# Second message-passing layer of a graph network: keys spread by a product on TensorE instead of a broadcast load

## The reference

```python
h = relu(layernorm(x))
for W, b, act in ((W1, b1, relu), (W2, b2, identity)):      # two message-passing layers
    fwd = segment_sum(h[src], dst) / max(deg_in, 1)
    bwd = segment_sum(h[dst], src) / max(deg_out, 1)
    h = act(concat([h, fwd, bwd]) @ W + b)
x = x + h
h   = relu(layernorm(x))
agg = segment_sum(edge_attr, dst)
z   = leaky_relu(concat([h, agg, u[0]]) @ w1 + b1m)
z   = leaky_relu(z @ w2 + b2m)
return x + z @ w3 + b3
```

## Time and profile before

| | |
|---|---|
| median of 3 runs | 4373.18 us (4371.87 to 4374.36) |
| the profiled execution's own time | 4380.62 us |
| span of its profile | 4378.9 us |
| mean granted clock of TensorE | 0.943 |

### The profile page before, as it was taken

The page is one execution under the profiler, slowest core; times in us unless marked ns, Lnnn a source line. Parts: engine busy times, 40 slices in busy tenths (PEclk is TensorE's granted clock), DMA queues, the critical chain, the costliest instruction groups (busy, mean ns, idle before and its releaser), DMA issues.

```text
span 4378.9 us, 97133 instructions
## 1 busy us (share of the span) xinstructions
PE 3723.8 (85%) x24424; PEld 3237.1 (74%) x24424; DVE 3174.5 (72%) x10907; ACT 2181.6 (50%) x5395; POOL 3251.1 (74%) x3256
## 2 busy tenths in 40 slices
PE   7999887788788857777677777599999999999999
PEld 5767677777777756666676666488888888888888
DVE  8999888888888823223232322399999999999998
ACT  6777533333333312222222222277777777777776
POOL 6777578888888778888888888666666666666665
PEclk9999899999999978888888888799999999999999
DMA  8999766666666668888888888766666666666664
GB/s 234 264 263 266 217 151 152 157 152 153 156 155 156 129 162 202 197 200 205 201 203 196 202 205 196 163 132 134 134 134 134 134 134 134 134 134 134 134 134 99
DMA packets 973215, 742.15 MB, mean 169 GB/s; under 512 B 192386, under 2 KB 834890, under 8 KB 973178
## 3 DMA queue, kind: packets, MB, share of 16 engines
q1 hardware_dynamic: 731706, 574.62, 44.0%
q0 software_dynamic: 241472, 167.10, 27.7%
HBM read 431.94 MB, written 309.52 MB: 169 GB/s over the span
## 4 chain that ended last, share of the span: by engine, by line
PE 41%; issue 22%; POOL 12%; DVE 12%; DMA 7%; SPq 2%; another core or an unknown queue 1%; ACT 1%; DVEq 1%; POOLq 0%; ACTq 0%
PE bank L1405 8%; POOL pre L555 6%; PE bank L1420 4%; PE bank L1418 4%; PE bank L1419 4%; DMA ends<-pre,index 3%; DVE stats L857 3%; POOL ends L576 2%; PE bank L1378 2%; PE bank L1382 2%; PE bank L1383 2%; PE bank L1379 2%; PE bank L1380 2%; PE bank L1392 2%; POOL ends L540 2%
## 5 line engine op out<-in xcount | busy, mean ns | idle before, releaser
L555 POOL DMA_INDIRECT pre<-summed,rep_index x392 | 620.9, 1584 | 155.4 <-issue 119.3
L591 POOL DMA_INDIRECT node<-summed,rep_index x392 | 624.4, 1593 | 131.2 <-issue 110.7
L622 POOL TENSOR_TENSOR resid<-node_out,b3s 128x128 f32<-128x128 f32 x784 | 337.6, 463 | 486.0 <-DVE rows L1142 482.4
L790 ACT ACTIVATE small<-bank,bias_small 128x512 f32<-128x512 f32 x784 | 534.9, 682 | 109.4 <-PE bank L1383 62.9
L1054 DVE TENSOR_SCALAR same<-keyall,keys 128x512 f32<-128x512 f32 (+3 forms) x392 | 138.5, 414 | 586.7 <-DMA keyall<-keyrow 467.5
L1095 DVE SCALAR_TENSOR_TENSOR z<-bank,bias,small 128x512 f32<-128x512 f32 x784 | 549.0, 740 | 14.5 <-ACT small L790 9.6
L632 POOL TENSOR_TENSOR z_lo<-z,z_hi 128x512 fp32r<-128x512 f32 x392 | 496.0, 1287 | 15.1 <-ACT z_hi L822 15.1
L745 ACT ACTIVATE endsT<-bank,b1col 128x512 f32<-128x512 f32 x98 | 67.4, 687 | 829.1 <-PE bank L1294 537.1
L576 POOL DMA_INDIRECT ends<-pre,index x392 | 381.5, 973 | 124.2 <-issue 118.8
L1203 PE MATMUL bank<-upper,table 112*128 112x256 bf16 x2744 | 340.7, 285 | 139.2 <-DVE upper L942 137.3
L1203 PEld LDWEIGHTS bank<-upper,table 112*128 112x128 bf16 x2744 | 273.0, 102 | 197.8 <-DVE upper L942 154.8
(11 more groups left out here) (144 smaller groups left out, 9948.7 us busy)
## 6 DMA issues: line engine op xcount, KB each, us to landing
node<-blank SPq DMA_DIRECT2D x98, 768.0 KB
node_out<-node SPq DMA_DIRECT2D x196, 384.0 KB, 3.5
rows<-in_x_dram SPq DMA_DIRECT2D x196, 256.0 KB
pre<-node_out SPq DMA_DIRECT2D x196, 256.0 KB
rows<-pre SPq DMA_DIRECT2D x196, 256.0 KB
normed<-in_x_dram SPq DMA_DIRECT2D x196, 256.0 KB
y<-node_out SPq DMA_DIRECT2D x196, 256.0 KB
node_out<-y POOLq DMA_DIRECT2D x196, 256.0 KB, 4.6
```

The lines of the kernel that those rows point to most:

```text
L555: pool.indirect_dma_start(pre1, bass.IndirectOffsetOnAxis(ap=rep_index[:, b, s:s + 1], axis=0), summed[:, b, s, 0:F], None, compute_op=ALU ...
L591: pool.indirect_dma_start(node1, bass.IndirectOffsetOnAxis(ap=rep_index[:, b, s:s + 1], axis=0), summed[:, b, s, :], None, compute_op=ALU. ...
L790: act.activation(small[:, m, :], bank[first_bank + m][:], ACT.Identity, scale=SLOPE, bias=bias_small[:, m:m + 1]).then_inc(ready, 1)
```

## The change

`keyall` and the DRAM row `keyrow` go, with the store that filled the latter at the start. SP loads the two `digit_rows` of the group (2 KB) in the place where `keyall` was loaded, with semaphore `c_rows`. PE gets `spread_keys(g + 1)` as the first thing of its step, ahead of `sums(g)`; it waits for that load and for `same` of group g, and writes bank 3. DVE compares from bank 3. Since bank 3 is taken, both node transposes of a group use bank 2, and the second waits until ScalarE has copied the first (`c_hT`). One semaphore of the weight split is merged into another (`s_split`), which waits for the same steps. Cut to its core:

```diff
@@ sync: layer 2 loads
-                        sp.wait_ge(c_same, g - 1)
-                    sp.dma_start(keyall[:, b, :], keyrow[bass.ds(g, 1), :].to_broadcast([P, GS])).then_inc(c_keyall[b], 16)
+                        sp.wait_ge(c_keys, g - 1)
+                    sp.dma_start(digit_rows[0:2, b, :], hilorow[bass.ds(g, 1)].rearrange("g d m -> (g d) m")).then_inc(c_rows[b], 16)
@@ scalar: node_rows
-                    act.activation(hT[:, 2 * b + i, 0:T, :].rearrange("p s f -> p (s f)"), bank[2 + i][:], ACT.Relu,
+                    act.activation(hT[:, 2 * b + i, 0:T, :].rearrange("p s f -> p (s f)"), bank[2][:], ACT.Relu,
@@ vector: same_as
-                    dve.wait_ge(c_keyall[b], 16 * uses)
+                    dve.wait_ge(c_keys, g + 1)
...
-                        last = dve.tensor_scalar(same[:, b, s, s * P:GS], keyall[:, b, s * P:GS],
+                        last = dve.tensor_scalar(same[:, b, s, s * P:GS], bank[3][:, s * P:GS],
@@ tensor: layer 2
+                def spread_keys(g, b, uses):
+                    pe.wait_ge(c_rows[b], 16 * uses)
+                    if before(g, 1):
+
+                        pe.wait_ge(c_same, g)
+                    pe.matmul(bank[3][:], places[:], digit_rows[:, b, :], start=True, stop=True).then_inc(c_keys, 1)
...
-                    if before(g, 1):
-
-                        pe.wait_ge(c_hT, g * 2 + i - 1)
+                    if i == 1 or before(g, 1):
+
+                        pe.wait_ge(c_hT, g * 2 + i)
                     for s in range(T):
-                        last = pe.transpose(bank[2 + i][:, s * P:(s + 1) * P], rows[:, 2 * b + i, s, :], ident[:])
+                        last = pe.transpose(bank[2][:, s * P:(s + 1) * P], rows[:, 2 * b + i, s, :], ident[:])
...
                     follows = not isinstance(g, int) or g + 1 < G
+                    if follows:
+                        spread_keys(g + 1, 1 - b, uses + b)
                     sums(g, b, uses)
```

More of the change, by code:

```diff
@@ L60, in gnn_kernel @@
     y1 = nc.dram_tensor("y1", (N, F), F32, kind="Internal").ap()
-    keyrow = nc.dram_tensor("keyrow", (G, GS), F32, kind="Internal").ap()
     hilorow = nc.dram_tensor("hilorow", (G, 2, GS), F16, kind="Internal").ap()
@@ L146, in gnn_kernel @@
             group_msg = own("group_msg", [P, 2, 4, ROW])
-            keyall = own("keyall", [P, 2, GS])
             same = own("same", [P, 2, 4, GS])
@@ L181, in gnn_kernel @@
         s_idsf = sem("ids_as_floats")
-        s_keyrow = sem("keyrow_stored")
         s_keysT = sem("keys_transposed")
@@ L220, in gnn_kernel @@
         c_endmm, c_msg = sem("c_end_products"), sem("c_messages_scaled")
-        c_keyall, c_attr = ([sem(f"c_{n}_loaded{b}") for b in range(2)] for n in ("keys", "edge_attr"))
+        c_rows, c_attr = ([sem(f"c_{n}_loaded{b}") for b in range(2)] for n in ("digit_rows", "edge_attr"))
+        c_keys = sem("c_keys_spread")
         c_same, c_repindex = sem("c_same_written"), sem("c_scatter_index_ready")
@@ L235, in gnn_kernel @@
         e_z1hi, e_z1lo = sem("e_z1_hi"), sem("e_z1_lo")
-        s_whi, s_split = sem("weights_rounded"), sem("weights_split")
+        s_split = sem("weights_rounded_and_split")
         e_L2, e_small2, e_z2 = sem("e_L2"), sem("e_small2"), sem("e_z2")
@@ L321, in _ @@
                          zeros[0:(NR - N) // 8, :].rearrange("p (r f) -> p r f", f=F)).then_inc(s_zeroed, 16)
-            sp.wait_ge(s_idsf, 1)
-            sp.dma_start(keyrow, ids[:]).then_inc(s_keyrow, 16)
             sp.wait_ge(s_hilo, 1)
@@ L366, in layer1 @@
                 sp.wait_ge(s_hilorow, 16)
-                sp.wait_ge(s_keyrow, 16)
                 sp.wait_ge(s_blank, 2)
@@ L1034, in _ @@
             for w, hi, _ in pairs:
-                dve.tensor_copy(hi[:], w[:]).then_inc(s_whi, 1)
-            dve.wait_ge(s_whi, len(pairs))
+                dve.tensor_copy(hi[:], w[:]).then_inc(s_split, 1)
+            dve.wait_ge(s_split, len(pairs))
             for w, hi, lo in pairs:
@@ L1351, in step @@
                         node_products(g, b, i)
+                spread_keys(0, 0, 1)
                 end_transposes(0, 0, 1)
@@ L1422, in tick @@
                         last.then_inc(e_L2, 1)
-            pe.wait_ge(s_split, 3)
+            pe.wait_ge(s_split, 6)
             ticks(pe, tick, 4)
```

## The result

The changed kernel takes 4592.06 us (median of 6 runs, 4587.57 to 4599.36) against 4371.68 us (4369.28 to 4374.36, 6 runs): ratio 1.0503, 95% interval 1.0492 to 1.0514. It is slower by 220 us.

The account below looks back on a forecast made before the run. GpSimd's indirect DMAs bound layer 2 at 12.7 us per group; TensorE's loop would replace them: 9.10 + 0.6 + 0.38 + 3.77 = 13.85, plus 0.35 clock, 14.2 us. Over 97 borders +145, less 5: 4513 us, range 4425 to 4645.

Parts of the forecast that it names:

- GpSimd sets the pace of before, broadcast and VectorE's wait are hidden: Layer 2 before: GpSimd's indirect DMAs give 12.7 us per group; removing the 256 KB broadcast and VectorE's 5.8 us wait gains nothing.
- Comparison out of PSUM, shared bank, key product by themselves cost nothing beside GpSimd: Layer 2 additions: comparison about 0.5 us more, beside the sums; second node transpose waits nothing; key product +0.38 us on TensorE.
- The chain through TensorE, VectorE, SP and the load: Between groups, TensorE idles from last product through addition, second store and digits load; its loop of 13.85 us exceeds GpSimd's 12.70.
- The gap, 3.77 us: TensorE's idle time ahead of the key product per group: 0.73 addition + 1.04 SP + 2.0 us load.
- The key product, 0.38 us: One added fp16 product per group on TensorE, 379 ns as in layer 1.
- Waits for ScalarE, 0.6 us: TensorE's waits for ScalarE within each layer 2 group, estimated at 0.6 us and said to stay whatever the pace.
- The clock, +0.35 us: Added to TensorE's 13.85 us group for the longer idle lowering its granted clock, giving 14.2 us.
- bound for that case: TensorE's group with all at 2.4 GHz: 3.11 sums + 5.59 + 0.38 + 3.77 = 12.85 us.
- the load was not as late as the broadcast: Rival 1: load lands as late as the broadcast did; gap 6.5 us, period 16.9 us, 4775 us; chance 0.09.
- the clock did not stay up: Rival 3: clock stays at 2.4 GHz, GpSimd stays the bound, no change: 4373 to 4383 us; chance 0.07.
- nothing got faster by fewer bytes: Rival 4: 0.26 MB less per group speeds GpSimd up by 1.2 us per group, 4255 us; chance 0.04.
- Rival 2: TensorE's clock falls in every group before the sums: period 15.5 us or somewhat above, 4640 up to 4670 us; chance 0.12.

Follow-up runs that it names:

- experiment 4: Kernel of before with the broadcast load of the keys left out except once per buffer, so later groups are compared with wrong keys: 4374.31 us, ratio 1.0003.
- experiment 1: Changed kernel with the digits (`digit_rows` load) issued one group earlier, ahead of the next group's loads: 4364.99 us, ratio to before 0.9981.
- 2: Changed kernel with the load still late but the key product placed behind the sums instead of ahead of them: 4366.70 us, ratio to before 0.9986.
- 3: Kernel of before with only the node transposes moved into one shared bank, bank 2: 4372.13 us, ratio 1.0001.
- 5: Changed kernel with the digits of group g+2 issued ahead of group g's second store, behind the wait for VectorE's second addition: 4389.00 us, ratio to before 1.0036.
- 7: Changed kernel with the digits issued two transfers later, behind the two loads of edge attributes: 4663.00 us, ratio to before 1.0666.
- experiment 9: Changed kernel with eight unneeded filling products on TensorE ahead of the key product: 4549.13 us, ratio to before 1.0388.
- experiment 6: Changed kernel with four unneeded filling products on TensorE ahead of the key product: 4391.74 us, ratio to before 1.0035.

## Why the prediction was right, and where its numbers were off

The forecast was 4513 us, slower, from a TensorE loop of 14.2 us; measured are 15.1 us between 1700 and 2500 us and 4592 us.

- *GpSimd sets the pace of before, broadcast and VectorE's wait are hidden*: right, shown by experiment 4 (no change without them) and by experiment 1 (GpSimd's 0.3 us gaps return).
- *Comparison out of PSUM, shared bank, key product by themselves cost nothing beside GpSimd*: right, experiments 1 to 3.
- *The chain through TensorE, VectorE, SP and the load becomes the bound*: right, shown by cutting it in two different ways (1, 2), shortening it (5) and lengthening it (7).
- *The gap, 3.77 us*: 4.11 measured. The addition and SP were as taken (0.7 and 1.1 us); the load took 2.2 us in the border shown, and 4.11 less 0.7 and 1.1 leaves 2.3 us on average, not 2.0. With only one store ahead of it (experiment 5) it took 1.7 us. The section of the Trainium skill that the prediction quotes for this (about 2.0 us of fixed cost) is written for transfers that GpSimd issues, while SP issues this one; 2.2 us would agree with it, the 1.7 us do not.
- *The key product, 0.38 us*: 0.56 (29.6 us over 53). It stands right behind the gap: the border shown has 0.61 us for it, where experiment 9, at a clock of 1.00, has 0.38.
- *Waits for ScalarE, 0.6 us*: 1.02 (35.5 + 18.4 us over 53), the largest of the misses. The split of before was right: experiments 3 and 4 have 0.63 us per group. What was wrong is that these waits stay whatever the pace. In the changed kernel the low clock lies elsewhere, the end products take 288 ns each and not 387, ScalarE's copy of the ends is as long as before (0.69 us), and TensorE stands at its waits sooner. The changed kernel and experiments 5, 6 and 7, all with 288 ns, have 1.0 us; experiments 1 to 4, with 362 to 368 ns, have 0.6. That this is the reason is argued from these rows, not tried.
- *The clock, +0.35 us*: the other matmuls went from 9.10 to 9.98 - 0.56 = 9.42 us, +0.32. The size agrees, but by luck: no row was behind the 0.35. It is the difference of two larger moves: the sums went from 3.12 to 5.07 us, and the other matmuls from 5.98 to 4.35. What I did not see is what the clock means once TensorE is the bound: before, half speed cost nothing, now it is all on the path. At full clock the loop would take 12.9 us and the change nearly nothing, as experiment 6 shows. The prediction's bound for that case was 12.85 us, though its gap was 0.4 us too short and its matmuls and waits together as much too long. So the change's loss is two things that are only large together: a chain that just uses up the slack, and the half clock that comes with this chain over the longest matmuls of the group. The mean clock of the stage (0.85 before, 0.84 after) hardly shows this. By an estimate from these means the lower level holds for 3.8 us of a group before and 4.8 after; what changed most is that it now lies on the sums.

The four differences, +0.34, +0.18, +0.42 and -0.03, make 0.9 us per group, 88 us over 97 borders; the median was off by 79. The rest is rounding: 53 whole groups in 800 us give 2.39 us more per group than before, while the 223 us of the whole layer give 2.3.

Of the rivals, three did not come true: the load was not as late as the broadcast (4.8 us), the clock did not stay up, and nothing got faster by fewer bytes. Rival 2, the clock that falls in every group before the sums, came true in part. In all 53 groups of the stretch the sums took over 4.0 us against 3.11 at full clock, but only in 19 of them 5.6 us or more; on average 5.07, between 3.11 and the 5.79 that the rival takes. So the measured 4592 us lie nearer to its 4640 than to my 4513, and 0.12 was little for it. The rule of the Trainium skill quoted in the prediction (page "TensorE: Matmul & The Clock Gate", section "HAM oscillation": a transfer wait in every turn of a loop can throttle the clock again in every turn) agrees with the trace more than I gave it credit for: period 15.1 us, nearer to its 15.5 than to my 14.2. Experiment 6, which keeps TensorE at work through most of the wait, gave 200 us.

The best version is experiment 1: the change with the digits loaded one group earlier, 0.19% faster than before. The runs in which GpSimd sets the pace (1, 2, 3, 4) all lie within 10 us of each other, with or without the broadcast, so more would have to come from GpSimd's indirect DMAs; that was not tried.

## What to carry to other kernels

A small load is not a cheap load when it is issued behind the stores of the last turn and the first matmul of the next turn waits for it: ask of every load what its issue depends on, and whether that depends on its own consumer. Price a new wait on TensorE together with the clock that follows it; filling the gap with useless products tells in one run how much of the loss is clock. And a wait that the list of waits puts high (VectorE's for the keys, 5.8 us per group) can be worth nothing: look first for the engine that has no waits at all.

## What the hardware showed that I had not expected

- Shortening TensorE's idle time by 1.46 us per group shortened the period by 2.19 us (experiment 5): the granted clock rose from 0.84 to 0.89 with it.
- 2.7 us of useless products per group made the kernel 200 us faster than without them (4391.7 against 4592.1 us), at a granted clock of 1.00 with 1.45 us of idle per group left. With 2.63 us left it was 0.94.
- In experiment 9 ScalarE started up to 1.4 us late behind transposes that the trace shows as done, in somewhat under half of the groups, and no view shows a reason. The profile of the kernel before has it too, those of experiments 3 and 4, with nearly the same kernel, do not.
